# Four graph layers on one core: the inverse root of two layer norms moved from GpSimd to VectorE

## The chip, the cores and the metric

The kernel runs on one core of a Trainium2 chip. The metric is the device time of one execution in microseconds (us). The program is one launch with all four graph layers in it.

## What is computed

Four message-passing layers on 6250 nodes (160 features: 64 scalars and 32 vectors of 3) and 100,000 edges sorted by destination. Before each layer the node rows are normalised; the change is about how `1 / sqrt(v + eps)` is made for layers 1 and 2, and for a second norm inside layer 2. Cut to what matters:

```python
def _layernorm(x, axis=-1, eps=1e-05):
    m = jnp.mean(x, axis=axis, keepdims=True)
    v = jnp.var(x, axis=axis, keepdims=True)
    return (x - m) / jnp.sqrt(v + eps)

h = jnp.maximum(_layernorm(x), 0.0)
x = x + L0(h, ...)          # edge pass 0
h = jnp.maximum(_layernorm(x), 0.0)
x = x + L1(h, ...)          # edge pass 1
h = jnp.maximum(_layernorm(x), 0.0)
x = x + L2(h, ...)          # begins with a second norm of h (EPS = 1e-5):
#   s_n = (s - mean(s)) * rsqrt(var(s) + EPS) * gamma_s + beta_s
#   v_n = v / sqrt(mean(sum(v * v, -1)) + EPS) * gamma_v
h = jnp.maximum(_layernorm(x), 0.0)
x = x + L3(h, ...)

# one edge layer (L0, L1, L3):
w   = act(act(edge_scalars @ Wfc1) @ Wfc2) @ Wfc3     # L1, L3: one hidden layer
mid = products of w, f[edge_src] and edge_attr
agg = segment_sum(mid, edge_dst)
out = linear maps of agg and of h, times node_attr
```

## The kernel before

**Edges.** The 100,000 edges are padded to 196 groups (`NG`) of 512 (`TG` = 4 tiles of 128). Nodes are 49 tiles (`NT`) of 128 rows, so about four groups of edges belong to one tile of nodes. Layers 0, 1 and 3 run through `edge_stream` (L789 on). Each engine has an in-order program of its own: `steps(eng, n, lag, emit, warm=36, unroll=4)` writes steps 0 to 35 out, then a hardware loop of four steps per turn, then the rest. A step has a number `i`, and its **slot** is `i % 4`. The engines are held together by counting semaphores alone.

In step `i` the engines do this, in this order:

- **GpSimd (POOL):** `own.pool`, then four indirect DMAs (L892), each gathering 128 source rows of group `i` out of the node table into one of four buffers. It may run up to four groups ahead of VectorE, since it waits for `made, (i - 3) * K`.
- **TensorE (PE):** hidden layer of group `i` (L913, `h`), weights of group `i - 1` (L920, `w`), in layer 0 a second hidden layer of group `i` (L926, `h2`), sums of group `i - 2` (L938, `win`), then `own.pe`. There is one PSUM bank for the hidden layers and one for the sums. `w` and `h` wait until ScalarE has finished the last hidden layer of the group before, `h2` until ScalarE has finished the first hidden layer of its group.
- **ScalarE (ACT):** the activation of group `i` (L966; in layer 0 two of them, after `h` and after `h2`), then `own.act`.
- **VectorE (DVE):** `add_window` of group `i - 2` (L757), in layer 0 the one-hot tiles (L992, L997; layer 1 reads them back from memory), the products of group `i` (L1002, L1006; they wait for the gathered rows and for `w`), then `own.dve`.

**The tail.** `own` is a class that does one node tile per four groups, its pieces spread over slots; `tile_of(i, s, r, slot, back)` says that a piece of tile `t` stands in slot `slot` of turn `t + back`. For layer 0 (`TailL0`), tile `t`:

- ACT gathers the sums (L1048: slot 0, back 3), PE maps them (L1071 to L1074: slot 1, back 3), DVE adds them to x and takes mean and variance (L1219, L1221, L764 to L769: slot 1, back 3).
- GpSimd raises the variance plus eps to the power -0.5 against a constant tile `half` that holds -0.5 (L1227: slot 0, back 4), **ahead of** the gathers of that step, and counts up `rooted`.
- ACT waits for `rooted` and makes bias (L1117), normalised rows (L1239), both slot 0, back 4, and then writes out the mapped rows of the tile before (L1248: slot 0, back 5).
- PE transposes them (L1156, L1157: slot 1, back 4) and maps them to the next layer's node table (L1162, L1163: slot 3, back 4); SP stores the rows.

Layer 1 (`TailL1`) is the same with more parts. Slot 1, back 3: five small DVE operations for an angle (L1313 to L1322). Slot 3, back 3: the update of x and the first norm's statistics (L1327 to L769). Slot 0, back 5: ACT makes h (L1377) and DVE takes the statistics of the second norm (L1337 to L1348, counted by `h_done`). The power (L1359: slot 2, back 4) is one operation on up to three columns: the first norm of tile `t` and the second norm (two columns) of tile `t - 1`, so GpSimd waits there for `done` and for `h_done` before it may gather on. ACT's readers stand in slots 3 and 0 behind it. Layer 3 has the same edge loop and a tail with no root.

## Time and profile before

| | |
|---|---|
| median of 3 runs | 6368.14 us (6365.52 to 6386.07) |
| the profiled execution's own time | 6384.29 us |
| its span | 6382.5 us |
| mean granted TensorE clock | 0.924 of full speed |
| PE busy | 5592.3 us (88%) |
| DVE busy | 4128.0 us (65%) |
| POOL busy | 4074.9 us (64%) |
| ACT busy | 2435.8 us (38%) |
| POOL, gathers of the edge layers (L892) | 2249.0 us busy in 2352 operations |

The span is the time from the first to the last instruction in the records; the execution's own time has 1.8 us around it. Layer 0's edge pass runs from about 160 to 1205 us of the span, layer 1's from about 1208 to 2340, layer 2 to about 4960, and layer 3 ends it. Shares of the whole span are averages over stages with different limits, so the stages that the change touches have to be read by themselves.

### The profile page before, as it was taken

What the parts mean: (1) busy time and instruction counts of PE and PEld (TensorE: products, weight loads), DVE (VectorE), ACT (ScalarE), POOL (GpSimd) and SP (SyncE); (2) the same over time, 40 slices, a digit from 0 to 9 for tenths busy, and PEclk for the clock granted to TensorE, in tenths of its full rate; (3) what the DMA queues carried; (4) which work ended last, traced back from release to release, by engine and by line L of the source; (5) the groups of instructions that cost most, each with busy time, mean ns of one, the idle gap of its engine ahead of it and who ended that gap; (6) DMA issues with size and microseconds to landing.
All of it is one profiled execution on the core that took longest, in us unless ns stands there. A gap on an engine that the chain in (4) does not pass through costs nothing. (4 is left out here: it accounts for less than half of the span.)

```text
span 6382.5 us, 222418 instructions
## 1 busy us (share of the span) xinstructions
PE 5592.3 (88%) x76769; PEld 4395.9 (69%) x76769; DVE 4128.0 (65%) x11379; ACT 2435.8 (38%) x6601; POOL 4074.9 (64%) x4031
## 2 busy tenths in 40 slices
PE   5898898788788859999999999999838879999998
PEld 3666666566666648888888888888727634777776
DVE  5566666345555547888888888888658775444443
ACT  3222222112222226777777777777600012111111
POOL 2777777577777746777777777777400012777776
PEclk9999999898888868999999999999869956999999
DMA  2444444455554533333333333333327502555554
GB/s 78 125 139 136 135 138 135 107 138 134 132 131 132 135 90 81 94 97 95 95 97 95 95 97 94 95 97 94 88 78 198 147 8 62 144 140 140 140 140 117
DMA packets 735477, 720.04 MB, mean 113 GB/s; under 512 B 249274, under 2 KB 594602, under 8 KB 734674
## 3 DMA queue, kind: packets, MB, share of 16 engines
q1 hardware_dynamic: 547154, 396.46, 21.8%
q0 software_dynamic: 188160, 321.38, 20.2%
q8 instruction: 106, 1.74, 0.1%
q14 instruction: 57, 0.47, 0.0%
HBM read 557.61 MB, written 159.75 MB: 112 GB/s over the span
## 5 line engine op out<-in xcount | busy, mean ns | idle before, releaser
L892 POOL DMA_INDIRECT l_edge_g<-node_table,l_edge_idx x2352 | 2249.0, 956 | 1003.3 <-issue 671.1
L938 PE MATMUL l_edge_win_ps<-l_edge_hot,l_edge_prod 128*32 128x40 f32 (+1 forms) x47040 | 1217.2, 227 | 300.8 <-issue 193.5
L938 PEld LDWEIGHTS l_edge_win_ps<-l_edge_hot,l_edge_prod 128*32 128x32 f32 x47040 | 1147.2, 116 | 462.6 <-issue 413.9
L966 ACT ACTIVATE l_edge_h<-l_edge_h_ps 128x256 f32<-128x256 f32 (+1 forms) x784 | 342.7, 437 | 2321.9 <-PE l_edge_h_ps L913 2098.2
L1002 DVE TENSOR_TENSOR l_edge_prod<-l_edge_w_ps,l_edge_g 128x512 f32<-128x512 f32 x588 | 406.1, 691 | 1216.4 <-DMA l_edge_g<-node_table,l_edge_idx 950.5
L1887 POOL DMA_INDIRECT att_g<-node_table,att_ends x784 | 896.6, 1144 | 286.1 <-issue 245.6
L1889 POOL DMA_INDIRECT att_g_dst<-node_table,att_ends x784 | 795.5, 1015 | 239.7 <-issue 239.7
L1909 PE MATMUL att_turn<-ident,sums_T 128*128 128x128 f32 (+1 forms) x4704 | 696.2, 284 | 38.0 <-ACT sums_T L1997 30.1
L1997 ACT ACTIVATE sums_T<-att_turn 128x512 f32<-128x512 f32 (+1 forms) x1176 | 662.8, 595 | 119.3 <-PE att_turn L1909 112.8
L920 PEld LDWEIGHTS l_edge_w_ps<-l_edge_wo,l_edge_h 64*128 64x128 f32 (+1 forms) x4704 | 501.3, 189 | 286.6 <-issue 244.1
L920 PE MATMUL l_edge_w_ps<-l_edge_wo,l_edge_h 64*128 64x192 f32 (+1 forms) x4704 | 676.8, 349 | 0.0
L1909 PEld LDWEIGHTS att_turn<-ident,sums_T 128*128 128x128 f32 (+1 forms) x4704 | 510.2, 142 | 198.0 <-issue 101.1
L1006 DVE TENSOR_TENSOR l_edge_prod<-l_edge_w_ps,l_edge_g 128x384 f32<-128x384 f32 x1176 | 594.5, 547 | 0.0
L913 PE MATMUL l_edge_h_ps<-l_edge_ea,l_edge_wi 16*128 16x256 f32 (+1 forms) x1176 | 495.3, 501 | 69.6 <-DMA l_edge_ea<-in_edge_attr_T 53.7
L757 DVE TENSOR_TENSOR sums_T<-sums_T,l_edge_win_ps 128x160 f32 x588 | 186.1, 316 | 242.8 <-issue 148.6
L1949 PE MATMUL att_o<-att_w_o2s,sums_T 128*128 128x96 f32 x1568 | 331.8, 294 | 12.9 <-ACT sums_T L1997 1.7
L2370 PE MATMUL sum_win_ps<-sum_hot,sum_prod 128*84 128x64 f32 x3136 | 275.4, 241 | 61.2 <-DVE sums_T L757 39.1
L1969 PEld LDWEIGHTS att_o<-att_w_o1v,sums_T 128*128 128x128 f32 x1568 | 257.4, 195 | 95.4 <-issue 95.1
L2370 PEld LDWEIGHTS sum_win_ps<-sum_hot,sum_prod 128*84 128x84 f32 x3136 | 251.9, 156 | 85.3 <-DVE sums_T L757 40.5
L1970 PE MATMUL att_o<-att_w_o1v,sums_T 128*128 128x64 f32 x1568 | 307.1, 278 | 0.0
L1953 PE MATMUL att_o<-att_w_o2v,sums_T 128*128 128x64 f32 x1568 | 306.9, 278 | 0.0
L1969 PE MATMUL att_o<-att_w_o1v,sums_T 128*128 128x64 f32 x1568 | 296.3, 271 | 0.0
(281 smaller groups left out, 9319.8 us busy)
## 6 DMA issues: line engine op xcount, KB each, us to landing
l_edge_hot<-hot_tiles SPq DMA_DIRECT2D x392, 320.0 KB
hot_tiles<-l_edge_hot SPq DMA_DIRECT2D x196, 320.0 KB
l_messages<-att_rows SPq DMA_DIRECT2D x196, 320.0 KB, 2.8
sum_msg<-l_messages SPq DMA_DIRECT2D x196, 320.0 KB, 3.5
l_edge_g<-node_table,l_edge_idx POOLq DMA_INDIRECT x2352
att_g<-node_table,att_ends POOLq DMA_INDIRECT x784
att_ea<-in_edge_attr_T SPq DMA_DIRECT2D x196, 64.0 KB
att_g_dst<-node_table,att_ends POOLq DMA_INDIRECT x784
```

The source lines that it names most:

```text
L892: pool.indirect_dma_start(g[s][:, t, :], None, rows_of, bass.IndirectOffsetOnAxis(idx[s][:, t:t + 1], 0)).then_inc(fetched[s], 16)
L913: nc.tensor.matmul(h_ps[0:HALVES * hid, 0:HC], wi[:, :], ea[s0][:, :]).then_inc(hidden[0], 1)
L920: ins = nc.tensor.matmul(w_ps[s1][:, m * (TG // HALVES) + n, 0:wn], h[last][s1][m * hid:(m + 1) * hid, n * P:(n + 1) * P], wo[m * hid:(m + ...
L938: return nc.tensor.matmul(win[n * VC:(n + 1) * VC, block * W:(block + kinds) * W], q[:, t, lo:lo + VC], to[:, t, kind:kind + kinds, :], st ...
L1002: nc.vector.tensor_tensor(halves[:, :, :, 0:SC], w[:, :, 0:2 * SC].rearrange("p t (n f) -> p t n f", n=2), rows[:, :, 0:SC].unsqueeze(2).t ...
L1006: ins = nc.vector.tensor_tensor(q[:, :, lo:lo + VF].rearrange("p t (c u) -> p t c u", c=XYZ), w[:, :, VS + n * VC:VS + (n + 1) * VC].unsqu ...
L1887: pool.indirect_dma_start(g[s][:, t, :], None, table[2], bass.IndirectOffsetOnAxis(ends[s][:, t:t + 1], 0)).then_inc(fetched[s], 16)
L1889: pool.indirect_dma_start(g_dst[s][:, t, :], None, table[3], bass.IndirectOffsetOnAxis(ends[s][:, TG + t:TG + t + 1], 0)).then_inc(fetched ...
L1909: ins = nc.tensor.transpose(turn[bank][0:width, t * P:(t + 1) * P], f[:, t, at:at + width], ident[:, :])
L1969: nc.tensor.matmul(o1[:, t, Q:PV + VC], feat_T[0][:, 1, e], w_o1v[0][:, :])
L1997: nc.scalar.activation(feat_T[n][0:width, part, :], turn[bank][0:width, :], ACT.Copy).then_inc(count, 1)
L2370: ins = nc.tensor.matmul(win_ps[s1][0:BW, b * SUM_WIN:(b + 1) * SUM_WIN], prod[s1][:, t, b, :], hot[s1][:, t, :], start=t == 0, stop=t == ...
```

## The change

The constant tile `half` and the two GpSimd powers go. A new function `NodeTail.root` makes the inverse root on VectorE: minus half of the variance, a first value from the bit pattern (shift right by one, subtract from 0x5F3759DF), and three Newton steps of three operations each, twelve operations in a chain that is held together by a new semaphore `refined`; the last one counts up `rooted`. It is called at the end of `own.dve` of the same slot and turn in which GpSimd did the power: slot 0, back 4 in layer 0, slot 2, back 4 in layer 1. ScalarE's, TensorE's and SP's programs are the same. `pool` of both tails does nothing.

```diff
+            def root(self, dve, at, lo, n):
+
+                var, y = self.of(self.var, at, lo, n), self.of(self.scale, at, lo, n)
+                m, a = self.minus_half[:, 0:n], self.step[:, 0:n]
+                k, count = at * self.KN, self.refined
+                at_least(dve, count, k)
+                nc.vector.tensor_scalar(m, var, -0.5, None, ALU.mult).then_inc(count, 1)
+                nc.vector.tensor_scalar(y.bitcast(I32), var.bitcast(I32), 1, None, ALU.arith_shift_right).then_inc(count, 1)
+                dve.wait_ge(count, k + 2)
+                nc.vector.tensor_scalar(y.bitcast(I32), y.bitcast(I32), -1.0, float(0x5F3759DF), ALU.mult, ALU.add).then_inc(count, 1)
+                for j in range(3):
+                    dve.wait_ge(count, k + 3 * j + 3)
+                    nc.vector.tensor_tensor(a, y, m, ALU.mult).then_inc(count, 1)
+                    dve.wait_ge(count, k + 3 * j + 4)
+                    nc.vector.tensor_tensor(a, a, y, ALU.mult).then_inc(count, 1)
+                    dve.wait_ge(count, k + 3 * j + 5)
+                    ins = nc.vector.scalar_tensor_tensor(y, a, 1.5, y, ALU.add, ALU.mult)
+                    ins.then_inc(count if j < 2 else self.rooted, 1)
...
         class TailL0(NodeTail):
...
                     stream_stats(dve, self.settled, k + 2, self.row(t), self.stat, self.mv, self.of(self.var, t), self.minus_mean[:, ds(t, 1)], self.done)
+                if (t := tile_of(i, s, r, 0, 4)) is not None:
+                    at_least(dve, self.done, (t + 1) * self.KD)
+                    self.root(dve, t, 0, 1)
 
             def pool(self, pool, i, s, r):
-                if (t := tile_of(i, s, r, 0, 4)) is not None:
-                    at_least(pool, self.done, (t + 1) * self.KD)
-                    nc.gpsimd.tensor_tensor(self.of(self.scale, t), self.of(self.var, t), self.half[:, 0:1], ALU.pow).then_inc(self.rooted, 1)
+                pass
...
         class TailL1(NodeTail):
...
-            def pool(self, pool, i, s, r):
                 t, former = tile_of(i, s, r, 2, 4), tile_of(i, s, r, 2, 5)
                 if t is not None or former is not None:
-                    at = t if t is not None else NT
                     lo, hi = 0 if t is not None else 1, 3 if former is not None else 1
                     if t is not None:
-                        at_least(pool, self.done, (t + 1) * self.KX)
+                        at_least(dve, self.done, (t + 1) * self.KX)
                     if former is not None:
-                        at_least(pool, self.h_done, (former + 1) * self.KH)
-                    nc.gpsimd.tensor_tensor(self.of(self.scale, at, lo, hi - lo), self.of(self.var, at, lo, hi - lo),
-                                            self.half[:, lo:hi], ALU.pow).then_inc(self.rooted, 1)
+                        at_least(dve, self.h_done, (former + 1) * self.KH)
+                    self.root(dve, t if t is not None else NT, lo, hi - lo)
+
+            def pool(self, pool, i, s, r):
+                pass
```

How the programs move, in three places of layer 0. First GpSimd at the beginning of a step of slot 0, before (names of semaphores that an earlier stage has freed are used again, so `setup_firsts` and the like stand for the edge layer's own counters; `l_tail_...` are the tail's tiles):

```order
L892 DMA l_edge_g<-node_table,l_edge_idx 128x160 [waits setup_firsts,l0_coef_ready,l0_zeroed]
L892 DMA l_edge_g<-node_table,l_edge_idx 128x160 x3
L1227 TENSOR_TENSOR l_tail_scale<-l_tail_var,l_tail_half 128x1 [waits l0_tail_done]
L892 DMA l_edge_g<-node_table,l_edge_idx 128x160 [waits setup_firsts,l0_cleared,l0_zeroed]
L892 DMA l_edge_g<-node_table,l_edge_idx 128x160 x3
```

With the change the row of L1227 is gone and the gathers follow each other. Second, VectorE at the end of the same step (the products of the group, then the next step's `add_window`), as a difference:

```order
 L1002 TENSOR_TENSOR l_edge_prod<-l_edge_w_ps,l_edge_g 128x8x64 [waits setup_iotas,l0_copied]
 L1006 TENSOR_TENSOR l_edge_prod<-l_edge_w_ps,l_edge_g 128x4x96 x2
+L1124 TENSOR_SCALAR l_tail_minus_half<-l_tail_var 128x1 [waits l0_tail_refined,l0_tail_done]
+L1125 TENSOR_SCALAR l_tail_scale<-l_tail_var 128x1
+L1127 TENSOR_SCALAR l_tail_scale<-l_tail_scale 128x1 [waits l0_tail_refined]
+L1130 TENSOR_TENSOR l_tail_step<-l_tail_scale,l_tail_minus_half 128x1 [waits l0_tail_refined]
+L1132 TENSOR_TENSOR l_tail_step<-l_tail_step,l_tail_scale 128x1 [waits l0_tail_refined]
+L1134 SCALAR_TENSOR_TENSOR l_tail_scale<-l_tail_step,l_tail_scale 128x1 [waits l0_tail_refined]
```

The last three of these rows come three times in all. The chain stands behind the products of the group, and those wait for `w` of that group, which TensorE issues in its next step. Third, ScalarE around the same place, with the change (L1138, L1260 and L1269 are L1117, L1239 and L1248 of before; the rows read the same before):

```order
L1048 ACTIVATE l_tail_sums<-sums_T 128x512 [waits l0_tail_posted,setup_made]
L1138 ACTIVATE l_tail_bias<-l_tail_minus_mean,l_tail_scale 128x1 [waits l0_tail_turned,l0_tail_rooted]
L1260 ACTIVATE l_tail_tile<-x,l_tail_bias,l_tail_scale 128x160 [waits l0_tail_biased,l0_tail_prep]
L1269 ACTIVATE l_tail_rows<-l_edge_node_ps,attr 128x320 [waits l0_tail_mapped]
L966 ACTIVATE l_edge_h_1<-l_edge_h_ps 128x256 [waits l0_stored2,l0_stored1]
```

Nothing moved there: the wait for `rooted` still stands ahead of the first hidden activation (L966) of the next step.

## Rows read from the trace of the kernel before

**Rows 1.** Busy time, PE clock and DMA by stretch: inside layer 0, inside layer 1.
```profile
240.00:1150.00 910.00, 821.26 (x16577) 619.72 (x16567) 565.81 (x1299) 239.78 (x649) 702.88 (x738) 0.98 0.48 136
1340.00:2290.00 950.00, 766.92 (x16076) 621.00 (x16075) 483.35 (x1591) 222.31 (x644) 694.95 (x732) 0.88 0.51 133
```

**Rows 2.** GpSimd in order of time (start us, us, ...), one power in layer 0.
```profile
506.50 0.95 POOL L892 DMA_INDIRECT l_edge_g<-node_table,l_edge_idx  x1 [0.30 <-issue]
507.47 0.83 POOL L1227 TENSOR_TENSOR l_tail_scale<-l_tail_var,l_tail_half 128x1 f32 x1
508.49 0.99 POOL L892 DMA_INDIRECT l_edge_g<-node_table,l_edge_idx  x1 [0.18 <-issue]
```

**Rows 3.** GpSimd in order of time: first and 46th power of layer 0.
```profile
232.93 0.59 POOL L1227 TENSOR_TENSOR l_tail_scale<-l_tail_var,l_tail_half 128x1 f32<-128x1 f32 x1
...
1177.91 0.80 POOL L1227 TENSOR_TENSOR l_tail_scale<-l_tail_var,l_tail_half 128x1 f32<-128x1 f32 x1
```

**Rows 4.** GpSimd in order of time: the second and the 45th power of layer 1.
```profile
1339.28 0.90 POOL L1359 TENSOR_TENSOR l_tail_scale<-l_tail_var,l_tail_half 128x3 f32<-128x3 f32 x1
...
2289.10 0.88 POOL L1359 TENSOR_TENSOR l_tail_scale<-l_tail_var,l_tail_half 128x3 f32 x1 [1.12 <-DVE l_tail_var L1348]
```

**Rows 5.** VectorE in order of time: the same place of two turns in layer 3.
```profile
5709.76 0.37 DVE L1474 SCALAR_TENSOR_TENSOR x<-l_edge_post_ps,l_tail_coef,x 128x160 f32 x1
...
5729.76 0.38 DVE L1474 SCALAR_TENSOR_TENSOR x<-l_edge_post_ps,l_tail_coef,x 128x160 f32 x1
```

**Rows 6.** TensorE in order of time, one turn of layer 0.
```profile
511.27 0.92 PE L920 MATMUL l_edge_w_ps<-l_edge_wo,l_edge_h 64*128 64x192 f32 x8
512.72 0.70 PE L926 MATMUL l_edge_h_ps<-l_edge_h,l_edge_wm 128*128 128x256 f32 x2 [0.52 <-ACT l_edge_h L966]
...
524.75 1.88 PE L938 MATMUL l_edge_win_ps<-l_edge_hot,l_edge_prod 128*32 128x120 f32 x80 [1.80 <-DVE sums_T L757]
```

**Rows 7.** ScalarE in order of time, slot 0 into slot 1 of layer 0.
```profile
509.65 0.28 ACT L1117 ACTIVATE l_tail_bias<-l_tail_minus_mean,l_tail_scale  x1
510.13 0.52 ACT L1239 ACTIVATE l_tail_tile<-x,l_tail_bias,l_tail_scale 128x160 f32 x1 [0.20 <-ACT l_tail_bias L1117]
511.86 0.53 ACT L1248 ACTIVATE l_tail_rows<-l_edge_node_ps,attr 128x320 f32<-128x320 f32 x1 [1.21 <-DMA l_self_rows<-l_tail_rows]
512.29 0.38 ACT L966 ACTIVATE l_edge_h<-l_edge_h_ps 128x256 f32<-128x256 f32 x1
```

**Rows 8.** VectorE in order of time, products of slot 0 in layer 0.
```profile
515.61 0.69 DVE L1002 TENSOR_TENSOR l_edge_prod<-l_edge_w_ps,l_edge_g 128x512 f32<-128x512 f32 x1 [3.22 <-DMA l_edge_g<-node_table,l_edge_idx]
```

**Rows 9.** VectorE in order of time, small operations and products in layer 1.
```profile
1712.03 0.15 DVE L1346 TENSOR_SCALAR l_tail_minus_mean_h<-l_tail_mv_h 128x1 f32 x1
1712.14 0.15 DVE L1348 TENSOR_SCALAR l_tail_var<-l_tail_var  x1
...
1716.47 0.69 DVE L1002 TENSOR_TENSOR l_edge_prod<-l_edge_w_ps,l_edge_g 128x512 f32<-128x512 f32 x1 [3.11 <-PE l_edge_w_ps L920]
...
1718.01 0.15 DVE L1313 SCALAR_TENSOR_TENSOR l_tail_turns<-l_edge_post_ps,l_tail_coef 128x1 f32<-128x1 f32 x1
...
1718.80 0.16 DVE L1322 TENSOR_TENSOR l_tail_turns<-l_tail_turns 128x2 f32<-128x2 f32 x1
1719.71 0.32 DVE L757 TENSOR_TENSOR sums_T<-sums_T,l_edge_win_ps 128x160 f32 x1 [0.75 <-issue]
```

**Rows 10.** TensorE in order of time: behind a gap in layer 1, and with none.
```profile
1709.41 3.38 PE L938 MATMUL l_edge_win_ps<-l_edge_hot,l_edge_prod 128*32 128x120 f32 x80 [4.25 <-issue]
...
1731.58 3.31 PE L938 MATMUL l_edge_win_ps<-l_edge_hot,l_edge_prod 128*32 128x120 f32 x80 [3.77 <-issue]
...
1737.71 1.91 PE L938 MATMUL l_edge_win_ps<-l_edge_hot,l_edge_prod 128*32 128x120 f32 x80
```

**Rows 11.** Busy time, PE clock and DMA in two-us stretches of layer 1.
```profile
1712.00:1714.00 2.00, 2.00 (x28) 1.91 (x24) 0.61 (x4) 0.00 (x0) 1.31 (x2) 0.50 0.24 49
1714.00:1716.00 2.00, 2.00 (x13) 1.29 (x13) 0.00 (x0) 0.38 (x1) 1.51 (x2) 0.85 0.71 195
```

More of the change, by code:

```diff
@@ L1083, in build @@
         class NodeTail(Tail):
-            OUTS_N, EXTRA = 1, 1
+            OUTS_N, EXTRA, KN = 1, 1, 11
             def make(self, ctx, tag):
@@ L1090, in make @@
                 self.mv = sbuf(ctx, f"{tag}_tail_mv", [P, 2])
-                self.half = sbuf(ctx, f"{tag}_tail_half", [P, 3])
+                self.minus_half = sbuf(ctx, f"{tag}_tail_minus_half", [P, 3])
+                self.step = sbuf(ctx, f"{tag}_tail_step", [P, 3])
+                self.refined = sem(ctx, f"{tag}_tail_refined")
                 self.var = sbuf(ctx, f"{tag}_tail_var", [P, NT + 1, 3])
@@ L1175, in build @@
         class TailL0(NodeTail):
-            KD, PREP = 6, 5
+            KD, PREP = 6, 4
             def more(self, ctx, tag):
@@ L1189, in dve_prep @@
                 nc.vector.memset(self.zeros[:, :], 0.0).then_inc(self.prep, 1)
-                nc.vector.memset(self.half[:, :], -0.5).then_inc(self.prep, 1)
                 nc.vector.tensor_scalar(self.coef[:, :], attr[:, 0, :], k, None, ALU.mult).then_inc(self.prep, 1)
-                dve.wait_ge(self.prep, 3)
+                dve.wait_ge(self.prep, 2)
                 nc.vector.tensor_tensor(self.coef[:, :], self.coef[:, :], self.coef[:, :], ALU.mult).then_inc(self.prep, 1)
@@ L1199, in dve_prep @@
                                         VC ** -0.5, None, ALU.mult).then_inc(self.prep, 1)
-                dve.wait_ge(self.prep, 5)
+                dve.wait_ge(self.prep, 4)
                 nc.vector.tensor_copy(self.w_v[:, VF:2 * VF], self.w_u[:, :]).then_inc(self.w_ready, 1)
@@ L1256, in build @@
         class TailL1(NodeTail):
-            KA, KX, KH, PREP = 5, 7, 9, 3
+            KA, KX, KH, PREP = 5, 7, 9, 2
             def more(self, ctx, tag):
@@ L1287, in dve_prep @@
                 nc.vector.memset(self.zeros[:, :], 0.0).then_inc(self.prep, 1)
-                nc.vector.memset(self.half[:, :], -0.5).then_inc(self.prep, 1)
                 nc.vector.tensor_scalar(self.coef[:, :], attr[:, 0, :], k, None, ALU.mult).then_inc(self.prep, 1)
@@ L1292, in dve_prep @@
                 nc.vector.tensor_scalar(self.w_v[:, :], self.w_v[:, :], self.gam[0:VF, 2:3], None, ALU.mult).then_inc(self.w_ready, 1)
-                dve.wait_ge(self.prep, 3)
+                dve.wait_ge(self.prep, 2)
             def pe_prep(self, pe):
```

## The prediction

> **What bounds the kernel now.** I read three views, in this order: busy time by stretch, the engines in order of time over one turn (four edge groups, one node tile) of each layer, and the clock in short stretches. In layer 0 TensorE is busy 821 of 910 us at clock 0.98, GpSimd 703 [rows 1]. Yet GpSimd sets the pace: its gathers follow each other with 0.30 us of issue between them and no other wait, and once a turn the power stands in between [rows 2]. A gather takes 0.95 + 0.30 = 1.25 us, sixteen of them 20.0 us; with the power, gather to gather is 508.49 - 506.50 = 1.99 us, 0.74 more. That makes 20.8, and the powers of layer 0 are (1177.91 - 232.93) / 45 = 21.0 us apart [rows 3]. TensorE idles (910 - 821) / (910 / 21.0) = 2.05 us a turn and so works 18.95; two of its waits in one turn were 0.52 and 1.80 us [rows 6]. VectorE waits for gathered rows, 3.22 us in slot 0 [rows 8].
>
> In layer 1 a turn is (2289.10 - 1339.28) / 43 = 22.09 us [rows 4]. GpSimd's power is 0.88 us there, and ahead of it GpSimd waits 1.12 us for VectorE's second norm [rows 4]: a loop GpSimd, gathers, products, statistics, power. Layer 3 has the same gathers and no power: its turn is 5729.76 - 5709.76 = 20.0 us [rows 5]. That is the floor that GpSimd leaves.
>
> **The new chain.** Twelve VectorE operations on one to three columns. The nearest rows are the angle's five operations, chained by the same kind of wait: four steps in 1718.80 - 1718.01 = 0.79 us, 0.20 each, the last 0.16 long [rows 9]. So the root takes 11 x 0.20 + 0.16 = 2.36 us. Its lower bound is 0.11 a step, as between two operations that hardly wait [rows 9]: 1.37 us. The upper bound, if the longer forms take 0.30 a step, is 3.5.
>
> A rule speaks to this. The Trainium skill (VectorE: DVE Perf Modes, "The DRAIN you can't avoid") says that a semaphore behind every chained operation costs nothing extra. The rows differ: 0.20 with the wait, 0.11 nearly without. By that rule the root would be 1.37 us and the total some 45 us lower than mine; I go by the row.
>
> **Layer 0: a gain on GpSimd, a stall on ScalarE.** The power's 0.74 us leave GpSimd. But the root is queued behind the products of its step i (slot 0), and those need `w` of group i, which TensorE issues in step i + 1. ScalarE, in step i, waits for `rooted` with the hidden activation of step i + 1 queued behind it, and TensorE needs that one for its `h2`, right behind `w`. Before, GpSimd ran ahead and had the root ready: ScalarE made the bias at 509.65 [rows 7], while the products of that step began at 515.61 [rows 8]. Now the order is forced, counted from the start of `w`:
>
> - `w` 0.92 [rows 6]; products start 0.04 later and the next VectorE operation 1718.01 - 1716.47 = 1.54 after them [rows 9]; root 2.36; signal 0.05. Sum 4.91.
> - ScalarE: bias to rows 510.13 - 509.65 = 0.48; rows 0.43; write-out to the next activation 512.29 - 511.86 = 0.43 (I take the same for the rows); activation to `h2` 512.72 - 512.29 = 0.43 [rows 6, 7]. The write-out's wait of 1.21 us for a store is over by then. Sum 1.77.
>
> So `h2` starts 6.68 us after `w` starts, and TensorE stands still for 6.68 - 0.92 = 5.8 us once a turn. Its own 18.95 us of work cannot lie under it. A turn at full clock is 18.95 + 5.8 = 24.7 us, more than GpSimd's 20.0: TensorE becomes the bound, and the gathers, four buffers ahead, no longer matter. VectorE's added chain itself is covered: VectorE now waits for TensorE.
>
> **The clock.** In layer 1 TensorE comes back from gaps of 4.25 and 3.77 us at the lower of its two levels: the sums take 3.38 and 3.31 us instead of 1.91 [rows 10], and the granted clock is 0.50 (1.2 GHz) from 1712 to 1714, on its way back to full in the two us behind [rows 11]. A gap of 5.8 us should do the same each turn. From 1709.41 to about 1714.3 are 4.9 us at the lower level, stretched by 3.38 / 1.91 = 1.77, so 2.1 us lost; the other gap recovered sooner. I take 2.0; the bounds are 0 (the level stays) and 2.6. A turn becomes 26.7 us: 5.7 x 45 turns = **+257 us**. In the drain three roots are on the path, each some 1.5 us longer than the power's 0.55: **+4**.
>
> **Layer 1.** ScalarE's readers of `rooted` stand one and two steps behind the root, not in its own step. TensorE's sums of that time wait anyway for `add_window`, which is queued behind the root, so ScalarE's wait is covered. GpSimd's loop is cut: floor 20.0. Do the others fit? VectorE: 483 us busy in 43 turns is 11.2 a turn [rows 1], the root 2.4, four issue gaps of 0.75 behind the tails [rows 9] 3.0, short waits inside the chains about 1: 17.6 us. TensorE: 767 us busy in 43 turns is 17.8 a turn, the slow clock included [rows 1]. The ring between both over two steps (`w` 0.96, products 1.54, issue gap 0.75, `add_window` 0.32, sums 1.91, `h` 0.6) is 6.1 us and is run through twice a turn, 12.2; the pieces of both tails that lie in it, the root among them, I estimate at 5: 17.2. All are under 20.0, by 2 us, so I take 20.2 with some jitter: 1.89 x 43 = **-81**. Bounds: -90 (the floor), and nothing gained or 0.3 a turn lost if VectorE's queue and slow TensorE stretches add up. In the drain five roots follow one another, each about 1 us longer: **+5**.
>
> The memset of `half` goes once in each layer, before the loop: nothing.
>
> **Sum.** 257 + 4 - 81 + 5 = +185 on the profiled execution's 6384.3 us: 6569. The profile lies 16.2 us above the median of the runs, so I predict 6368.1 + 185 = 6553, rounded to **6550 us**.
>
> **The rivals.**
>
> - *The stall comes, the clock stays* (chance 0.12). Both gaps seen speak against it; for it, that TensorE has `h` and `w` right ahead of the gap and is denser in layer 0. 45 x 2.0 less: 6460 us.
> - *The stall comes, and layer 1 gives nothing* (0.13). VectorE has 17.6 us of work in a 20 us turn, and TensorE and VectorE wait for each other twice a step. For it: the gap of 4.25 us before the sums hangs on VectorE's tail of slot 3, which stays. Layer 1 then keeps 22.1: 6550 + 81 = 6630 us.
> - *Faster: the stall does not bite* (0.07). If ScalarE got its root before TensorE needed the next activation, layer 0 would drop to GpSimd's floor: (21.0 - 20.1) x 45 = 40 us, with layer 1's 76 together -116: 6250 us. It decides at a stall of 2.05 - 0.9 = 1.15 us a turn; below that TensorE's idle time swallows it. For it speaks only that GpSimd's row is plainly the limiter; against it that the products alone, which the root must follow, start after `w`.
> - *In between* (0.04): a stall of about 3 us and no clock loss, 45 x (18.95 + 3 - 21.0) = +43 and -76: within 0.3% of before.
>
> **How the numbers follow.** Forecast 0.64, the rivals 0.12, 0.13, 0.07, 0.04. The forecast's own range is 6490 to 6610 (root 1.4 to 3.5 us: -45 to +50; clock 1.0 to 2.6: -45 to +27). Taking in the first two rivals gives 6450 to 6640; outside remain the two rivals under it and some spread. A measurement of this kernel tells about 0.3% (19 us) from no change: faster 0.07, same 0.04, slower 0.89.
>
> **What would show it.** In the profile after: in layer 0, ScalarE's bias (now L1138) waits for VectorE's L1134 once a turn, longest of ScalarE's waits after those for TensorE; TensorE's L926 of slot 1 idles 5 to 6 us for L966; the sums behind it take about 3.3 us at clock 0.5; the turn is 26 to 27 us; GpSimd's gathers wait for VectorE's products. In layer 1, gathers without a break and a turn near 20.2 us. Wrong would be: a turn of 20 us in layer 0 (no stall), of 24.7 (clock kept), of 22 or more in layer 1, or root steps far from 0.20 us.

## The result and the profile after

The changed kernel takes **6546.94 us** (median of 4 runs, 6542.45 to 6561.04) against 6367.54 (4 runs, 6365.52 to 6386.07): ratio 1.0279, 95% interval 1.0253 to 1.0304, so 179 us slower. The forecast was 6550. The profiled execution has 6561.04 us, 176.8 more than that of before.

In this part a turn is measured by the gathers, which number the groups without a gap: sixteen times their mean distance, over 624 gathers inside layer 0 and 608 inside layer 1.

| | before | after |
|---|---|---|
| turn of layer 0 | 21.02 us | 27.00 us |
| turn of layer 1 | 22.09 us | 20.20 us |
| first gather of layer 0 to first of layer 1 | 1076.6 us | 1355.5 us |
| first to last gather of layer 1 | 1086.3 us | 1004.9 us |
| from there to the end | 4083.5 us | 4062.9 us |

Layer 0 lost 278.9 us, layer 1 gained 81.4. The last stretch is 20.6 us shorter, and two things meet in it. Layer 1's last steps are longer with the change: its last root ends 47.6 us after its last gather, 35.7 before, so 11.9 are lost. From there on neither kernel changes a line, and that part took 4047.8 us before and 4015.4 after. In the profiles of the ten kernels of this document from such chips it lies between these two values, whatever the kernel, so up to 32 us of a difference between two profiles can come from there. The changed stages lost 278.9 - 81.4 + 11.9 = 209 us by the two profiles.

The page of the profile, engines and clock by 40 slices; slices 2 to 9 are layer 0:

```profile
PE 5641.3 (86%) x76769; PEld 4426.3 (67%) x76769; DVE 4305.3 (66%) x12565; ACT 2428.8 (37%) x6601; POOL 3993.6 (61%) x3932
...
PEclk9888888887999996999999999999969955999999
```

Busy time, clock and DMA inside layer 0 and inside layer 1 (columns as in [rows 1]):

```profile
240.00:1400.00 1160.00, 900.87 (x16238) 683.16 (x16238) 626.98 (x1791) 236.19 (x640) 667.05 (x688) 0.81 0.37 105
1630.00:2490.00 860.00, 721.07 (x15824) 578.00 (x15828) 558.24 (x2072) 215.96 (x639) 644.59 (x681) 0.94 0.54 145
```

TensorE's busy share of layer 0 fell from 90% to 78% and its clock from 0.98 to 0.81; in layer 1 the clock rose from 0.88 to 0.94. Where the time went shows in one turn of layer 0, engine by engine in order of time. TensorE:

```profile
616.30 0.92 PE L920 MATMUL l_edge_w_ps<-l_edge_wo,l_edge_h 64*128 64x192 f32 x8
623.32 1.22 PE L926 MATMUL l_edge_h_ps<-l_edge_h,l_edge_wm 128*128 128x256 f32 x2 [6.09 <-ACT l_edge_h L966]
624.47 3.42 PE L938 MATMUL l_edge_win_ps<-l_edge_hot,l_edge_prod 128*32 128x120 f32 x80
627.82 0.90 PE L1071 MATMUL l_edge_post_ps<-l_tail_w,l_tail_sums 128*128 128x161 f32 x2
```

ScalarE:

```profile
614.22 0.62 ACT L1048 ACTIVATE l_tail_sums<-sums_T 128x512 f32 x1
621.56 0.29 ACT L1138 ACTIVATE l_tail_bias<-l_tail_minus_mean,l_tail_scale  x1 [6.71 <-DVE l_tail_scale L1134]
622.06 0.52 ACT L1260 ACTIVATE l_tail_tile<-x,l_tail_bias,l_tail_scale 128x160 f32 x1 [0.20 <-ACT l_tail_bias L1138]
622.48 0.51 ACT L1269 ACTIVATE l_tail_rows<-l_edge_node_ps,attr 128x320 f32<-128x320 f32 x1
622.89 0.37 ACT L966 ACTIVATE l_edge_h<-l_edge_h_ps 128x256 f32<-128x256 f32 x1
```

VectorE:

```profile
616.17 0.32 DVE L757 TENSOR_TENSOR sums_T<-sums_T,l_edge_win_ps 128x160 f32 x1 [1.23 <-PE l_edge_win_ps L938]
...
617.60 0.68 DVE L1002 TENSOR_TENSOR l_edge_prod<-l_edge_w_ps,l_edge_g 128x512 f32<-128x512 f32 x1
618.20 1.01 DVE L1006 TENSOR_TENSOR l_edge_prod<-l_edge_w_ps,l_edge_g 128x384 f32<-128x384 f32 x2
619.13 0.14 DVE L1124 TENSOR_SCALAR l_tail_minus_half<-l_tail_var 128x1 f32 x1
619.19 0.14 DVE L1125 TENSOR_SCALAR l_tail_scale<-l_tail_var  x1
...
619.55 0.16 DVE L1130 TENSOR_TENSOR l_tail_step<-l_tail_scale,l_tail_minus_half 128x1 f32<-128x1 f32 x1
619.75 0.16 DVE L1132 TENSOR_TENSOR l_tail_step<-l_tail_step,l_tail_scale 128x1 f32<-128x1 f32 x1
...
621.16 0.16 DVE L1134 SCALAR_TENSOR_TENSOR l_tail_scale<-l_tail_step,l_tail_scale 128x1 f32 x1
```

Read them together: TensorE writes `w` at 616.30, only then may VectorE make the products (617.60), behind these stands the root (619.13 to 621.32), only then ScalarE's bias (621.56), and the hidden activation (622.89) waits in its queue for three operations more. TensorE stands still for 6.09 us; over the 27 such places between 400 and 1120 us the mean is 5.97. When it comes back it runs at the lower level: 3.42 us for sums that take 1.91 [rows 10], in each of the 27.

In layer 1 the gathers (GpSimd, in order of time) come every 1.25 us. Only 11 gaps in 38 turns are longer, 0.5 to 1.5 us; this is one:

```profile
2013.15 0.95 POOL L892 DMA_INDIRECT l_edge_g<-node_table,l_edge_idx  x1 [0.30 <-issue]
2015.10 0.94 POOL L892 DMA_INDIRECT l_edge_g<-node_table,l_edge_idx  x1 [1.00 <-issue]
```

ScalarE waits there for the root as well, and TensorE has two short gaps a turn (TensorE, ScalarE, in order of time):

```profile
2016.84 1.92 PE L938 MATMUL l_edge_win_ps<-l_edge_hot,l_edge_prod 128*32 128x120 f32 x80 [1.66 <-DVE sums_T L757]
...
2022.02 3.32 PE L938 MATMUL l_edge_win_ps<-l_edge_hot,l_edge_prod 128*32 128x120 f32 x80 [1.43 <-issue]
```

```profile
2015.67 0.29 ACT L1138 ACTIVATE l_tail_bias_h<-l_tail_minus_mean_h,l_tail_scale  x1 [4.29 <-DVE l_tail_scale L1134]
```

### The profile page after: what moved, and what is told of

Read it like the earlier page. It is cut to its first block and busy times, and to the rows that moved or that the text cites. A ratio compares the mean times of both kernels' runs of the same rounds, so it can differ in the third digit from the quotient of the medians.

```text
span 6559.4 us, 224474 instructions
## 1 busy us (share of the span) xinstructions
PE 5641.3 (86%) x76769; PEld 4426.3 (67%) x76769; DVE 4305.3 (66%) x12565; ACT 2428.8 (37%) x6601; POOL 3993.6 (61%) x3932
## 5 line engine op out<-in xcount | busy, mean ns | idle before, releaser
L938 PEld LDWEIGHTS l_edge_win_ps<-l_edge_hot,l_edge_prod 128*32 128x32 f32 x47040 | 1170.8, 118 | 365.5 <-issue 338.3
L938 PE MATMUL l_edge_win_ps<-l_edge_hot,l_edge_prod 128*32 128x40 f32 (+1 forms) x47040 | 1246.2, 230 | 183.0 <-issue 90.5
L966 ACT ACTIVATE l_edge_h<-l_edge_h_ps 128x256 f32<-128x256 f32 (+1 forms) x784 | 341.2, 435 | 2165.8 <-PE l_edge_h_ps L913 1932.6
L1906 POOL DMA_INDIRECT att_g<-node_table,att_ends x784 | 843.6, 1076 | 316.5 <-issue 316.2
L1908 POOL DMA_INDIRECT att_g_dst<-node_table,att_ends x784 | 850.1, 1084 | 238.9 <-issue 238.9
L913 PE MATMUL l_edge_h_ps<-l_edge_ea,l_edge_wi 16*128 16x256 f32 (+1 forms) x1176 | 495.9, 501 | 66.3 <-DMA l_edge_ea<-in_edge_attr_T 51.9
L926 PE MATMUL l_edge_h_ps<-l_edge_h,l_edge_wm 128*128 128x256 f32 x392 | 162.6, 502 | 269.0 <-ACT l_edge_h L966 269.0
L1989 PE MATMUL att_o<-att_w_o1v,sums_T 128*128 128x64 f32 x1568 | 304.8, 276 | 0.0
```

Source lines behind the costliest of these rows:

```text
L913: nc.tensor.matmul(h_ps[0:HALVES * hid, 0:HC], wi[:, :], ea[s0][:, :]).then_inc(hidden[0], 1)
L938: return nc.tensor.matmul(win[n * VC:(n + 1) * VC, block * W:(block + kinds) * W], q[:, t, lo:lo + VC], to[:, t, kind:kind + kinds, :], st ...
L966: nc.scalar.activation(h[n][s % 2][:, :], h_ps[0:HALVES * hid, 0:HC], act_fn, scale=scales[n]).then_inc(active[n], 1)
L1906: pool.indirect_dma_start(g[s][:, t, :], None, table[2], bass.IndirectOffsetOnAxis(ends[s][:, t:t + 1], 0)).then_inc(fetched[s], 16)
L1908: pool.indirect_dma_start(g_dst[s][:, t, :], None, table[3], bass.IndirectOffsetOnAxis(ends[s][:, TG + t:TG + t + 1], 0)).then_inc(fetched ...
```

## Experiment 1: one layer at a time

Layer 0's power goes back to GpSimd (`a2`), or layer 1's (`b2`); the other layer keeps the root. The core of the first, in `TailL0`; the second is the same in `TailL1`:

```diff
-                if (t := tile_of(i, s, r, 0, 4)) is not None:
-                    at_least(dve, self.done, (t + 1) * self.KD)
-                    self.root(dve, t, 0, 1)
...
+                    nc.gpsimd.tensor_tensor(self.of(self.scale, t), self.of(self.var, t), self.half[:, 0:1], ALU.pow).then_inc(self.rooted, 1)
```

> Layer 0's power is GpSimd's again, layer 1 keeps VectorE's root. Theory (the whole loss is layer 0's stall of 6.1 us and the clock behind it): layer 0 turns in 18.9 us as before, layer 1 in 20.3 us; about 6290 us, under the kernel before by the 73 to 81 us of layer 1. Rival (layer 1's gain comes only because the layer ahead of it is slower): about 6370. The same edit ran once on a chip on which the kernel before took 10646 us; there nothing could be told.

> Layer 1's power is GpSimd's again, layer 0 keeps VectorE's root where the change has it. Theory (layer 1 gains by itself what the gathers gain without the power): layer 1's turn is 22.1 us again, layer 0's stays 27.3; the time is the change's plus 73 to 90 us, about 6630. With layer 0's power back alone at 6282, the two edits should add up: (6282 - 6371) = -89 for layer 1, so 6547 + 89 = 6636. Rival (the layers' times depend on each other, or unchanged layers moved): under 6600 or over 6660.

Measured: `a2` **6282.24 us** (ratio to the kernel before 0.9867, 0.9839 to 0.9894), layer 0's turn 21.01, layer 1's 20.17 us. `b2` **6629.61 us** (1.0399, 1.0382 to 1.0416), turns 26.83 and 22.00. Both theories hold (the turn of 18.9 us that the first gives for layer 0 is wrong: it was 21.02 before). The ratios multiply to 0.9867 x 1.0399 = 1.026, beside the change's 1.028: the two layers' effects are separate, -89 us for layer 1 and +256 for layer 0. These are differences of whole times, so the stretch that varies by 32 us is in them. In the profiles layer 1 with its last steps gives -81.7 + 11.7 = -70 us in `a2`, and layer 0 gives +272 in `b2`. Half of the change, that of layer 1, is a version that beats both kernels.

## Experiment 2: is the slow clock a cost of its own?

Sixteen matmuls on the identity, into an unused part of a bank, stand between `w` and `h2` of the step that stalls. They produce nothing that is read. In the records each of them stands as two, so x32.

```diff
+                            if w_mid and live(i, NG) and tile_of(i, s, r, 1, 4) is not None:
+                                for _ in range(16):
+                                    nc.tensor.matmul(post_bank[:, 256:384], ident[:, :], ident[:, :])
                             if w_mid and live(i, NG):
```

> 16 matmuls of 128x128x128 into an unused part of a bank stand in layer 0's stall, between w and h2, so that TensorE is busy while it waits for ScalarE. They add no result. Theory (stall and clock are two separate costs): the sums behind the stall take 1.9 us in place of 3.4, the turn falls from 27.3 by 2 us to 25.3; about 6450 us. Rival (the sums are slow for another reason, or the fill is longer than the stall): sums stay at 3.4 us, 6550 or more.

Measured: **6457.91 us** (1.0133, 1.0107 to 1.0159), turn 24.73 us. TensorE in order of time:

```profile
610.96 3.84 PE L926 MATMUL l_edge_post_ps<-ident 128*128 128x128 f32 x32
617.09 0.70 PE L929 MATMUL l_edge_h_ps<-l_edge_h,l_edge_wm 128*128 128x256 f32 x2 [2.29 <-ACT l_edge_h L969]
617.71 1.91 PE L941 MATMUL l_edge_win_ps<-l_edge_hot,l_edge_prod 128*32 128x120 f32 x80
```

3.84 us of fill and 2.29 of waiting are the same 6.1 us in which `h2` can't start, but what follows is fast: 0.70 in place of 1.22, 1.91 in place of 3.42. The turn is 27.00 - 24.73 = 2.27 us shorter, with more work in it. So the stall has two prices, 6 us of standing and at least 2.3 us of slow running behind it, and the second is the gap's, not the wait's. The fill did not take away all of it: behind 9 of 29 stalls the sums still took 2.6 to 3.2 us, as here:

```profile
441.46 2.77 PE L941 MATMUL l_edge_win_ps<-l_edge_hot,l_edge_prod 128*32 128x120 f32 x80
```

The whole price can be estimated from rows at either level: `h2` 1.22 for 0.70, sums 3.42 for 1.91, and the four maps behind them (L1071 to L1074) 2.08 for 1.37 in the mean, together 2.7 us.

## Experiment 3: a longer root

Six Newton steps in place of three, in both layers.

```diff
-                for j in range(3):
+                for j in range(6):
```

> Six Newton steps in both layers in place of three: nine more VectorE operations of 0.195 us each a turn, 1.75 us. The result is the same root. Theory (in layer 0 the root lies on the path once a turn, from w to h2): layer 0's turn grows by 1.75 us, 27.3 to 29.0, +79 us over 45 turns. Layer 1: VectorE delays add_window, which TensorE's sums await there by 1.66 us already, so up to 1.75 a turn more, 0 to +77. 6625 to 6705. Rival (in layer 0 something other than the root's length ends the wait): layer 0's turn grows by less than 1 us.

Measured: **6767.34 us** (1.0613, 1.0595 to 1.0631), turns 28.05 and 22.98 us: over the range. TensorE, the stall of layer 0 and the gap of layer 1:

```profile
639.34 1.22 PE L926 MATMUL l_edge_h_ps<-l_edge_h,l_edge_wm 128*128 128x256 f32 x2 [7.55 <-ACT l_edge_h L966]
640.49 2.80 PE L938 MATMUL l_edge_win_ps<-l_edge_hot,l_edge_prod 128*32 128x120 f32 x80
...
2115.10 3.41 PE L938 MATMUL l_edge_win_ps<-l_edge_hot,l_edge_prod 128*32 128x120 f32 x80 [3.58 <-DVE sums_T L757]
```

In layer 0 the mean stall is 7.65 us, 1.68 more than 5.97, which is the nine operations nearly one to one: the root is on the path. The turn grows by only 1.05, as what stands behind the stall is now partly fast again: the sums take 3.18 us in the mean, from 2.72 to 3.42, and the four maps 1.58 in place of 2.08. Why is not shown. In layer 1 the expectation missed: the gap before the sums grows from 1.66 to 3.58 us, and now brings the lower level with it (3.41 in place of 1.92; 74 of 167 groups of sums took over 2.5 us, with three steps 29 of 170), so the turn grows by 2.78, more than the work added. Layer 1's gain stands on a root that is short. Of the 206 us between the two profiles layer 0 has 49, layer 1 with its last steps 128; some 29 lie in the stretch that neither kernel changes.

## Experiment 4: the root in another place

`c2`: layer 0's root two steps earlier in the tile's course, behind slot 2's products. `g`: that, and layer 1's root from slot 2 to slot 0, two steps earlier as well (the second piece of the diff).

```diff
-                if (t := tile_of(i, s, r, 0, 4)) is not None:
+                if (t := tile_of(i, s, r, 2, 3)) is not None:
                     at_least(dve, self.done, (t + 1) * self.KD)
                     self.root(dve, t, 0, 1)
...
-                t, former = tile_of(i, s, r, 2, 4), tile_of(i, s, r, 2, 5)
+                t, former = tile_of(i, s, r, 0, 4), tile_of(i, s, r, 0, 5)
```

> Layer 0's root stands one slot earlier, behind slot 2's products, where VectorE has nothing urgent behind it; layer 1 as in the change. Theory (the place of the root, not its 2.2 us, makes the stall): ScalarE's bias doesn't wait, sums_T and h2 come on time, layer 0's turn is at most 18.9 us, with GpSimd's 0.74 us a turn gained 18.2; 6260 to 6290 us. Rival (VectorE's 2.2 us and its eleven operations a turn are too much wherever they stand): the turn stays over 20 us, above 6340.

> Layer 0's root behind slot 2's products, and layer 1's moved from slot 2 to slot 0 of its turn, behind the statistics, where VectorE idles 0.75 and 2.28 us. Theory (layer 1 loses 1.66 + 1.43 us of TensorE's turn, and the half clock behind it, to ScalarE's wait of 4.3 us for the root): layer 1's turn falls from 20.3 to 18.0 to 19.0 us, so 60 to 110 us less than the kernel with layer 0's root early alone; 6150 to 6220. Rival (layer 1 is bound by GpSimd's gathers, 1.25 us each, 15 in 18.75 us plus loop): nearly nothing, 6240 to 6280.

Measured: `c2` **6367.31 us** (1.0001, 0.9986 to 1.0016), turns 22.69 and 20.08; `g` **6420.76 us** (1.0071, 1.0048 to 1.0093), turns 22.70 and 21.77. Both theories missed (the 18.9 us that layer 0's theory starts from is wrong here too: the turn before is 21.02). `c2` lies where its rival put it, over 20 us and above 6340, but the rival's cause, VectorE's 2.2 us wherever they stand, does not survive experiment 5. In `c2` the wait for the root is gone and the turn is 4.3 us shorter, but another wait has come. ScalarE and TensorE in order of time:

```profile
629.30 0.53 ACT L1269 ACTIVATE l_tail_rows<-l_edge_node_ps,attr 128x320 f32<-128x320 f32 x1 [3.90 <-DMA l_self_rows<-l_tail_rows]
```

```profile
630.15 0.83 PE L926 MATMUL l_edge_h_ps<-l_edge_h,l_edge_wm 128*128 128x256 f32 x2 [2.35 <-ACT l_edge_h L966]
```

VectorE's selectors, and SyncE's queue (SPq):

```profile
624.67 0.82 DVE L997 TENSOR_TENSOR l_edge_hot<-l_edge_here,y 128x640 f32<-128x640 f32 x1
```

```profile
625.67 0.35 SPq L871 DMA_DIRECT2D hot_tiles<-l_edge_hot  x1
626.31 0.35 SPq L1189 DMA_DIRECT2D node_table<-l_tail_rows  x1
626.76 0.40 SPq L1189 DMA_DIRECT2D l_self_rows<-l_tail_rows  x1
```

The rows' store (L1189) is queued on SyncE behind the write of the selectors, which waits for VectorE's L997, and this the root pushed back by its 2.2 us. ScalarE needs the store's end before it may overwrite the rows; before, that wait was 1.21 us [rows 7]. The hidden activation that was late behind the root is now late behind the store.

In `g` ScalarE no longer waits for layer 1's root, and the turn is 1.7 us longer than in `c2`: statistics and root follow each other in one slot of VectorE's queue, and TensorE's sums wait 2.03 us for the `add_window` behind them in place of 1.66 (TensorE in order of time):

```profile
2017.42 1.90 PE L938 MATMUL l_edge_win_ps<-l_edge_hot,l_edge_prod 128*32 128x120 f32 x80 [2.03 <-DVE sums_T L757]
```

The longer waits ahead of the sums are 0.6 us a turn, and more groups of sums run at the lower level (39 of 168, in `c2` 28); the rest of the 1.7 us was not traced. So ScalarE's 4.3 us in layer 1, a large wait in the profile, were not what made TensorE's gaps; the longest piece of VectorE's queue between two `add_window` fits them better. Whether that wait costs anything where VectorE's queue stays as it is, this run can't tell, since it changed both.

## Experiment 5: root and store early

`c2`, and SyncE stores the tail's rows one slot earlier (`TailL0.sp`):

```diff
-                if (t := tile_of(i, s, r, 2, 6)) is not None:
+                if (t := tile_of(i, s, r, 1, 6)) is not None:
                     self.store(sp, t, [table[1], self_rows])
```

> The early root of layer 0 (behind slot 2's products), and SyncE's store of the tail's rows in slot 1 of its turn in place of slot 2, so that it isn't queued behind the write of the selectors that VectorE now makes 2.2 us later. In the run with the root early alone ScalarE waited 3.9 us a turn for that store, with the hidden activation behind it, and layer 0's turn was 22.9 us. Theory (the delay runs from VectorE's root through its selectors and SyncE's queue to ScalarE): that wait is gone, TensorE's L926 doesn't idle 2.4 us for it, the sums behind take 1.9 us, layer 0's turn falls to 20.0 to 20.6 us; 6240 to 6270, faster than the kernel with GpSimd's power in layer 0 (6282). Rival (TensorE waits then for VectorE's add_window, the other thing that the root delays): the turn stays over 22 us, 6330 or more.

Measured: **6286.75 us** (0.9859, 0.9843 to 0.9876), turns 21.03 and 20.18. ScalarE's wait for the store and TensorE's for L926 are gone, layer 0 is 1.66 us a turn faster than in `c2`: the chain from root to selectors to SyncE to ScalarE is what held it. But the turn isn't 20.0 to 20.6. `k` is level with `a2`, whose intervals overlap its own, although GpSimd here has no power left in layer 0 and none of its gaps between gathers is over 0.32 us from the 80th gather to the layer's last. The 0.74 us went into the gathers themselves. GpSimd's group of gathers in layer 0, 300 to 1100 us (count, busy us, mean ns, idle), of the kernel before and of `k`:

```profile
L892 POOL DMA_INDIRECT l_edge_g<-node_table,l_edge_idx x611 | 589.4, 965 | 181.5 <-issue 148.1 <-DVE l_tail_minus_mean L769 10.4 <-DVE l_edge_here L992 10.4
```

```profile
L892 POOL DMA_INDIRECT l_edge_g<-node_table,l_edge_idx x607 | 615.3, 1014 | 184.9 <-issue 164.5 <-DMA l_edge_idx<-in_src_groups 10.7 <-DVE l_edge_prod L1006 5.8
```

(1.014 + 0.30) x 16 = 21.0, the turn. Which gathers are long shows in order of time, GpSimd and then VectorE:

```profile
612.03 1.42 POOL L892 DMA_INDIRECT l_edge_g<-node_table,l_edge_idx  x1 [0.30 <-issue]
613.75 0.95 POOL L892 DMA_INDIRECT l_edge_g<-node_table,l_edge_idx  x1 [0.31 <-issue]
615.00 1.39 POOL L892 DMA_INDIRECT l_edge_g<-node_table,l_edge_idx  x1 [0.30 <-issue]
```

```profile
611.80 0.83 DVE L997 TENSOR_TENSOR l_edge_hot<-l_edge_here,y 128x640 f32<-128x640 f32 x1
...
614.76 0.82 DVE L997 TENSOR_TENSOR l_edge_hot<-l_edge_here,y 128x640 f32<-128x640 f32 x1
```

A gather that begins while L997 runs is stretched. Between 400 and 820 us of `k`, 58 gathers began inside an L997: mean 1.31 us, 52 over 1.1. Of 52 in which an L997 began, and of 209 that don't touch one, none. (The expectation of experiment 6 has 59, from rounded times.) In the kernel before, 48 gathers began inside an L997 and only 5 were over 1.1 us (mean 0.99).

What decides is when in L997 the gather begins. Those that begin 0.05 to 0.69 us into it all end 0.81 to 0.87 us after its end, so the earlier they begin the longer they are: 1.42 us at 0.23, 1.39 at 0.24 in the rows above. Those in its last 0.13 us, and in its first 0.04, take 0.95. In `k` 55 of the 58 lie in the part that stretches, in the kernel before 7 of 48, and 36 in the last 0.13 us, like this one (GpSimd, then VectorE):

```profile
518.59 0.95 POOL L892 DMA_INDIRECT l_edge_g<-node_table,l_edge_idx  x1 [0.30 <-issue]
```

```profile
517.82 0.82 DVE L997 TENSOR_TENSOR l_edge_hot<-l_edge_here,y 128x640 f32<-128x640 f32 x1
```

So the kernel before escapes by its phase: its gathers mostly start as L997 ends. The Trainium skill has a rule for it (SBUF — State Buffer, "Who interferes with whom"): a VectorE instruction with two inputs in SBUF contends with a GpSimd one that reads SBUF, and who issues first keeps the port while the other waits. The rows of `k` agree for the gathers that come second. That VectorE waits when the gather came first they do not show: of 173 L997 between 240 and 1150 us of `k`, the 117 that began inside a gather took 0.83 us as the others did, and in the mean began no later behind the operation ahead of them.

## Experiment 6: the selectors with one input

`k`, with L997 as a copy of `here`. The selectors' weight `y` is left out, so this kernel computes unweighted sums; sizes and counts are the same.

```diff
-                                nc.vector.tensor_tensor(to[:, :, :, :], here[:, :, :].unsqueeze(2).to_broadcast([P, TG, 1 + XYZ, EDGE_WIN]),
-                                                        y.to_broadcast([P, TG, 1 + XYZ, EDGE_WIN]), ALU.mult).then_inc(made, 1)
+                                nc.vector.tensor_scalar(to[:, :, :, :].rearrange("p t c n -> p t n c"),
+                                                        here[:, :, :].unsqueeze(3).to_broadcast([P, TG, EDGE_WIN, 1 + XYZ]), 1.0, None, ALU.mult).then_inc(made, 1)
```

> The kernel with layer 0's root and store early, and in layer 0 the selectors' 128x640 multiplication (L997) reads one tensor of SBUF in place of two: the weight y is left out, so the selectors are copies; same size written, once a group. In the run with root and store early, GpSimd's gathers took 1.014 us in the mean against 0.965 in the kernel before, and of 59 that began inside an L997 52 took over 1.1 us (mean 1.30); of 261 others one did. That made layer 0's turn 21.1 us where 16 x 1.25 = 20.0 was expected. Theory (VectorE with two inputs in SBUF holds GpSimd's gather off until it ends, as the Trainium skill says of the shared port pair in SBUF - State Buffer, section 'SBUF: two separate sides'): no stretched gathers, mean 0.95, turn 20.0 to 20.3, 6235 to 6260. Rival (the gathers are long for another reason, the write of the selectors by SyncE or the rows' store): mean stays 1.01, turn 21.1, 6280 to 6295. If the copy keeps GpSimd off as well, the gathers that begin inside it show it in their lengths.

Measured: **6266.55 us** (0.9814, 0.9791 to 0.9837), turn of layer 0 20.61 us, between the two expectations. Gathers and L997, by group, 300 to 1100 us:

```profile
L892 POOL DMA_INDIRECT l_edge_g<-node_table,l_edge_idx x621 | 611.0, 984 | 189.3 <-issue 159.4 <-DVE l_edge_prod L1006 13.7 <-DVE l_edge_here L992 11.9
```

```profile
L997 DVE TENSOR_SCALAR l_edge_hot<-l_edge_here 128x640 f32<-128x640 f32 x155 | 120.2, 776 | 5.8
```

The mean gather is 0.984 us, and (0.984 + 0.30) x 16 = 20.5 is again close to the turn: gathers set the pace, and their length follows from what L997 is. But the copy keeps GpSimd off as well, half as much: of 49 that began inside it 26 took over 1.1 us (mean 1.12), of 58 in which it began 13, of 218 apart none. The expectation that one input clears the port fell for this form. Shown is that the stretch belongs to the overlap with L997 (in `k` none of the gathers of layer 0 that began outside an L997 took over 1.02 us); by which port or mode the copy does it stays open.

## On a second chip

The first four kernels (`a`, `b`, `c`, `d`, the same code as `a2`, `b2`, `c2`, `d2`) ran on a chip on which the kernel before itself takes 10646.34 us (14 runs, 10607.97 to 10675.17).

> Layer 0 has GpSimd's power again, layer 1 keeps the root on VectorE. Theory (layer 0 pays for a stall, layer 1 gains by GpSimd's cut loop): layer 0 is back at a turn of 21.0 us, layer 1 stays at 20.3, so about 6367 - 75 = 6290 us, faster than both kernels. Rival (VectorE's added operations cost in either layer): layer 1 would not be below 22.1 us a turn and the time not under 6360.

> Layer 1 has GpSimd's power again, layer 0 keeps the root on VectorE. Theory: layer 0 at 27.3 us a turn, layer 1 at 22.1: 6367 + 6.3 x 45 = about 6645 us, slower than the changed kernel by 75 to 100. Rival (the layers disturb each other, or the loss lies in both): the time is not the sum of the parts, under 6600.

> Both layers keep the root on VectorE; in layer 0 it is called in slot 2, back 3, two steps earlier, with the same twelve operations. Theory (only the place behind the products of ScalarE's own step costs): ScalarE's wait for rooted is gone, TensorE's 6 us gap too, a turn of layer 0 falls from 27.3 to GpSimd's floor, 20.1 to 20.6 us: 6367 - 0.7 x 45 - 75 = about 6260 us. Rival (the twelve operations overload VectorE or its ring with TensorE): a turn of 22 us or more, 6350 us or more.

> The changed kernel, with 16 matmuls of ident by ident into unused columns of a PSUM bank issued in each stall of layer 0, behind w and ahead of h2 (about 5 us of work in a gap of 6). Theory (the stall costs twice, the second time through TensorE's clock): the sums behind the stall take 1.9 instead of 3.4 us, a turn falls from 27.3 to about 25.1 us, 6547 - 2.2 x 45 = about 6450 us. Rival (the clock is no part of it, only the wait counts): no change or slower, 6547 us or more.

Ratios to the kernel before: `a` 1.0078 (1.0053 to 1.0102), `b` 1.0037 (1.0016 to 1.0059), `c` 1.0085 (1.0053 to 1.0118), `d` 1.0135 (1.0092 to 1.0179). None of the four expectations could be judged. Of `a`, busy time, clock and DMA in a part of layer 0, and TensorE in order of time in layer 1:

```profile
200.00:1200.00 1000.00, 673.18 (x9456) 473.52 (x9454) 322.52 (x732) 132.82 (x356) 403.13 (x425) 0.73 0.25 71
```

```profile
4001.99 0.24 PE L938 MATMUL l_edge_win_ps<-l_edge_hot,l_edge_prod 128*32 128x40 f32 x2 [0.52 <-issue]
4003.45 0.20 PE L938 MATMUL l_edge_win_ps<-l_edge_hot,l_edge_prod 128*32 128x40 f32 x1 [1.21 <-issue]
4004.87 0.90 PE L938 MATMUL l_edge_win_ps<-l_edge_hot,l_edge_prod 128*32 128x40 f32 x21 [1.23 <-issue]
```

TensorE stops for 0.5 and 1.2 us in the middle of a run of 80 matmuls that wait for nothing the profile shows, in every layer, and the mean clock over the span is 0.68. A gather takes 0.957 us there as elsewhere. `b`, 4% slower on the other chips, is 0.4% slower here; a stall of 6 us made by other engines may hide where TensorE is late anyway. That, and why TensorE stops there, is open. All other numbers of this document are from chips on which the kernel before takes 6367 to 6379 us.

## Why the prediction was right

**The stall.** Forecast from rows of before: `h2` 6.68 us after `w` starts, 5.8 us of idle TensorE. In the turn shown it is 7.02 and 6.09 us, in the mean of 27 places 6.89 and 5.97. By its terms: the products began 1.30 us after `w`, not 0.96, since `add_window` waited 1.23 us for TensorE and the selectors stood behind it; from products to root 1.53 (forecast 1.54); the root from 619.13 to 621.32, 2.19 (2.36); from there to the bias 0.24 (0.05, a signal that I took without a row); ScalarE's chain to `h2` 623.32 - 621.56 = 1.76 (1.77). The root was taken 0.17 too long, the rest 0.5 too short, so the misses cancel in part. Experiments 1 and 3 show cause and length: without the root there, no stall; with nine more operations, 1.68 us more of it.

**The root's price.** A step that waits for the one ahead comes every 0.195 us, two that don't wait (L1124, L1125) stand 0.06 apart. I took 0.20 from the angle's chain [rows 9]. The Trainium skill (VectorE: DVE Perf Modes, "The DRAIN you can't avoid") says that the semaphore costs nothing extra, measured there on eight copies; by that rule I had put the root at 1.37 us, and it is 2.19. The trace does not agree for operations this small, and the measurement decides for the row.

**The clock.** 2.0 us a turn in the forecast, bounds 0 and 2.6. The fill of experiment 2 gave back 2.27, and the whole price by the rows is about 2.7, just over the bound. The row of layer 1 that I took it from had 4.9 us at the lower level; here they are about 6, from 623.32 to the third of the four maps.

**Layer 0 in sum.** Turn 26.7 forecast, 27.00 measured; +261 with the drain forecast, +278.9 measured. Within the turn the stall was 0.2 us longer and the clock 0.7 dearer than forecast, and the work 18.3 us in place of 18.95 (27.00 - 5.97 - 2.7): my 18.95 was TensorE's busy share of before, which has slow stretches of its own (sums of 2.8 to 3.4 us in 9 of 138 groups). From the first to the last gather the layer lost 265 us, forecast 257; from there to the first gather of layer 1 it lost 49.4 - 35.7 = 13.7, and I had 4 for the drain.

**Layer 1.** Turn 20.2 forecast, 20.20 measured; -81 forecast, -81.4 measured with all of the layer's gathers; the drain +5 forecast, +11.9 measured. That ScalarE's wait there is covered agrees with `g`, where it is gone and the turn isn't shorter, but isn't shown apart from VectorE's queue. That VectorE's root has room there is true by a small margin, as the six steps show.

**A wrong step.** The forecast said that GpSimd's gathers would wait for VectorE's products. They waited 242.1 us for the load of their indices, and 47.3 for the products (layer 0, 240 to 1400 us). SyncE issues that load behind the load of the edge attributes, which waits for TensorE's hidden layer L913 (699.6 us in 170 waits there). It cost the sum nothing. Deeper is what "GpSimd sets the pace" left out: I took a gather as 0.95 us whatever else runs, and the rival "the stall does not bite" would by that have given 6250 us. `k` is that case, the stall gone and the power gone, and it gave 6287, since gathers that begin inside L997 took back what the power had cost.

**Luck.** 6547 beside 6550 is closer than the terms were. By the two profiles the changed stages lost 209 us where the sum had 185; the two drains alone were 26 in place of 9. The 32 us by which the unchanged stretch was shorter in the second profile take that back. The mechanism of layer 0, the wait, the path and the clock, is what experiments 1 to 3 bear out; the last 20 us of the agreement are luck.

**The rivals.** "The clock stays" (6460) is what `d2` made of the change, 6458: it was right about the price and not about the case. "Layer 1 gives nothing" (6630) is the time of `b2`, 6630.

## What to carry to other kernels

Before an operation moves to another engine, write down behind what it will stand in that engine's queue, and who waits for it with what behind: the root is 2.2 us long and cost 6 of standing and over 2 of slow running, as it was put behind products that themselves needed a step of TensorE's that ScalarE then held up. Taking one such wait away shows the next; follow it through every queue, the DMA queue too, until the pace is set by an engine that never waits. Adopt a change by layers: here one half was worth -89 us and the other +256 by the whole time.

## What was not expected of the hardware

- Gathers issued by GpSimd lengthen from 0.95 to 1.1 to 1.6 us when they begin 0.05 to 0.69 us into VectorE's 128x640 multiplication of two SBUF tensors (52 of the 58 that begin inside it in `k`, 5 of 48 in the kernel before, where most begin at its end), and less often inside a copy of the same size (26 of 49).
- TensorE came back at the lower level even after short gaps: in layer 1 the sums took 3.32 us behind gaps of 1.66 and 1.43 us with work between them, and 1.92 behind the first of the two. Behind the second of these gaps 22 of 36 groups of sums took over 2.5 us, behind the first 3 of 38. A longer stall (7.65 in place of 5.97 us) left less slow running behind it, not more.
- On one chip TensorE paused 0.5 and 1.2 us inside runs of matmuls, and the same program took 1.67 times as long.
